# The second expert layer of a decoder: rows fetched by a table of places in place of rows scattered to slots

## The reference

```python
idx1 = jnp.argmax(gates, axis=-1)
mask1 = jax.nn.one_hot(idx1, nE)
idx2 = jnp.argmax(gates * (1.0 - mask1), axis=-1)
mask2 = jax.nn.one_hot(idx2, nE)
pos1 = jnp.cumsum(mask1, axis=0) - mask1
mask1 = mask1 * (pos1 < capacity)
pos2 = jnp.cumsum(mask2, axis=0) - mask2 + jnp.sum(mask1, axis=0, keepdims=True)
mask2 = mask2 * (pos2 < capacity)
...
expert_in = jnp.einsum('nec,nh->ech', dispatch, x)
hmid = jax.nn.silu(jnp.einsum('ech,ehf->ecf', expert_in, w1) + b1[:, None, :])
expert_out = jnp.einsum('ecf,efh->ech', hmid, w2) + b2[:, None, :]
y = jnp.einsum('nec,ech->nh', combine, expert_out)
shared = jax.nn.silu(x @ sw1 + sb1) @ sw2 + sb2
out = y + SHARED_SCALE * shared
```

## Time and profile before

| | |
|---|---|
| Time, median of 3 runs (lowest, highest) | 1610.15 us (1605.52, 1614.38) |
| The profiled execution: its time, its span | 1613.86 us, 1611.9 us |
| Busy share of the span: PE, PEld, DVE, ACT, POOL | 90%, 69%, 64%, 51%, 42% |
| Share of the chain that ended last, L2245 (the 28 scatters) | 8.8% of the chain's view by line |
| Span of the stage `experts1` | about 187 us, from 1425 us to the end |

### The profile page before, as it was taken

The page is one execution under the profiler, slowest core; times in us unless marked ns, Lnnn a source line. Parts: engine busy times, 40 slices in busy tenths (PEclk is TensorE's granted clock), DMA queues, the critical chain, the costliest instruction groups (busy, mean ns, idle before and its releaser), DMA issues. The chain is left out here.

```text
span 1611.9 us, 43113 instructions
## 1 busy us (share of the span) xinstructions
PE 1453.4 (90%) x16061; PEld 1116.6 (69%) x16061; DVE 1037.6 (64%) x1692; ACT 827.6 (51%) x1297; POOL 672.4 (42%) x732
## 2 busy tenths in 40 slices
PE   7988899989999987679999999999999999985684
PEld 4445676679999656357777777777777777764583
DVE  4334545668788559467777777777777777535362
ACT  5553333432222337436666666666666666654461
POOL 2300000477787546444433444334443344147263
PEclk9879999999999999789999999999999999987797
DMA  2064984131110320285556655666556655331402
GB/s 78 23 173 136 241 240 131 40 110 63 65 42 23 55 51 2 61 199 116 129 141 153 136 129 127 143 153 134 129 127 143 153 133 129 83 80 38 110 25 85
DMA packets 72884, 174.36 MB, mean 108 GB/s; under 512 B 14989, under 2 KB 44286, under 8 KB 72800
## 3 DMA queue, kind: packets, MB, share of 16 engines
q1 hardware_dynamic: 67936, 157.72, 40.1%
q10 hardware_dynamic: 2688, 11.78, 2.5%
q0 software_dynamic: 2176, 3.71, 0.7%
HBM read 87.58 MB, written 9.56 MB: 60 GB/s over the span
## 5 line engine op out<-in xcount | busy, mean ns | idle before, releaser
L2006 DVE TENSOR_REDUCE hat_tops<-banks 128x1 f32<-128x500 f32 x672 | 439.3, 676 | 153.1 <-PE banks L1751 153.0
L1879 ACT ACTIVATE hat_pb<-banks 125x896 f32<-125x896 f32 x384 | 340.3, 916 | 226.5 <-PE banks L1770 222.7
L1751 PE MATMUL banks<-hat_kh,hat_qm 128*128 128x500 f32 x672 | 298.1, 462 | 5.7 <-DVE hat_tops L2006 3.5
L1770 PEld LDWEIGHTS banks<-hat_q,hat_k 128*125 128x125 f32 x1536 | 219.8, 189 | 74.8 <-issue 32.4
L1770 PE MATMUL banks<-hat_q,hat_k 128*125 128x224 f32 x1536 | 250.8, 286 | 16.2 <-ACT hat_pb L1879 9.2
L1948 POOL CAST hat_kh<-hat_kf 128x500 fp32r<-128x500 f32 x96 | 58.5, 609 | 404.3 <-ACT hat_kf L1892 388.3
L1761 PE MATMUL banks<-hat_pb,hat_vs 125*27 125x168 f32 (+1 forms) x6144 | 166.9, 261 | 0.1
L1761 PEld LDWEIGHTS banks<-hat_pb,hat_vs 125*27 125x27 f32 (+1 forms) x6144 | 132.2, 98 | 43.9 <-issue 24.4
L1751 PEld LDWEIGHTS banks<-hat_kh,hat_qm 128*128 128x128 f32 x672 | 127.8, 192 | 47.4 <-DVE hat_tops L2006 32.8
L1315 ACT ACTIVATE ffn_rg<-banks 128x448 f32<-128x448 f32 x128 | 69.9, 546 | 166.2 <-PE banks L1248 166.0
L1954 POOL TENSOR_TENSOR hat_kl<-hat_kf,hat_kh 128x500 fp32r<-128x500 f32 x96 | 118.2, 1258 | 2.1 <-DMA hat_k<-hat_kh 2.1
(11 more groups left out here) (338 smaller groups left out, 2721.8 us busy)
## 6 DMA issues: line engine op xcount, KB each, us to landing
hat_k<-hat_kh SPq DMA_DIRECT2D x256, 187.5 KB, 4.8
hat_ct<-ctxT SPq DMA_DIRECT2D x32, 750.0 KB, 6.1
hat_k<-hat_kl SPq DMA_DIRECT2D x128, 187.5 KB, 4.5
ctx_cx<-ctx SPq DMA_DIRECT2D x32, 672.0 KB
ctx_cd<-ctxT ACTq DMA_DIRECT2D x15, 750.0 KB, 5.0
ffn_cb<-expert_weights SPq DMA_DIRECT2D x8, 896.0 KB, 4.4
moe_raw<-Mw SPq DMA_DIRECT2D x18, 256.0 KB, 4.0
ctx_cx<-ctx SPq DMA_DIRECT2D x32, 78.0 KB
```

Source lines behind the costliest of these rows:

```text
L1751: peak_out.inc(nc.tensor.matmul(g.bank(PK + m % 2)[:, 0:SB], qm[u][:].rearrange("p h i -> p (h i)")[:, r * 128:r * 128 + 128], kh[u][:, c ...
L1770: mm = nc.tensor.matmul(g.bank(2 * (t % 2) + j // 2)[0:SW, (j % 2) * QW:(j % 2 + 1) * QW], k3[u][:, j, t * SW:(t + 1) * SW], q3[u][:, j, : ...
L1879: exped.inc(nc.scalar.activation(pb[t % 6][:].rearrange("p (n i) -> p n i", n=2), g.ps[0:SW, 2 * (t % 2):2 * (t % 2) + 2, 0:2 * QW], ACT.E ...
L2006: peaked.inc(v.tensor_reduce(tops[:, r, n:n + 1], g.bank(PK + m % 2)[:, 0:SB], AX_X, ALU.max))
```

## The change

- The rows of tokens are stored once to memory (`rows`, 4 transfers of SyncE, in its queue behind the loads of the third set of weights), and GpSimd fetches an expert's rows straight from there by a list of token numbers, 128 rows an instruction: four instructions an expert and one more for each pair of experts, which holds the last 48 rows of both. That is 36 fetches in place of 28 scatters and 8 loads, and 36 sends in place of 40.
- The list is a table of places, made by matmuls. `on_pe_tally` sums each tile's choices, ScalarE copies the sums (`by_tile`), `on_pe_places` makes the places of both choices (six matmuls in place of VectorE's running sums), VectorE makes for each of the 28 tiles and choices a 128 by 128 matrix of zeros and ones (`lanes`, four instructions of 896 columns) and 36 columns of numbers (`tile_of`), and `on_pe_list` multiplies and adds up all 28. VectorE makes the numbers to fetch and to send from the sum (`name`).
- GpSimd's list: rows of experts 0 to 3, then in round e the results of e, then the rows of e+4. There are four buffers of rows (`ROWS`); the fetch of e+4 waits for `turn(e)`.
- TensorE's list: logits are made chunk by chunk inside the norm; six pieces up of the shared expert stand ahead of the list matmuls, and all 16 pieces down behind them, each with the piece up six further on.
- VectorE takes over from GpSimd the remainders of the first four pieces and of the stream (`low_x`), and gives to ScalarE the diagonals of shares (`lots`, 28 instructions of 128 columns, four in each round from 1 on, behind the round's other work). Copying an expert's rows out of PSUM takes one instruction on ScalarE and on VectorE instead of two, and `keep_out` two instead of one.
- Weights have four sets of buffers instead of six; two sets that were rounded during the shared expert are rounded in rounds 1 and 2. The rows loaded back at the end have four buffers, so no load waits for a matmul. Clearing `slot_rows` in an earlier stage goes away, and the constants are 292 columns wider.

```diff
+    def on_pe_tally(self, pe, bank):
         nc = self.g.nc
-        pe.wait_ge((self.one, self.two)[k], 1)
-        flat = self.hot[:, k].rearrange("p t e -> p (t e)")
-        nc.tensor.matmul(bank[:, 224 * k:224 * k + 112], self.g.c["before"], flat, start=True, stop=True)
-        nc.tensor.matmul(bank[:, 224 * k + 112:224 * k + 224], self.g.c["ones"], flat, start=True, stop=True).then_inc(self.tallied, 1)
+        pe.wait_ge(self.taken, 2)
+        for k in range(2):
+            flat = self.hot[:, k].rearrange("p t e -> p (t e)")
+            mm = nc.tensor.matmul(bank[0:TT * E, k * 128:k * 128 + 128], flat, self.g.c["ones"], start=True, stop=True)
+        mm.then_inc(self.summed, 1)
+
+    def on_act_tally(self, act, bank):
+        act.wait_ge(self.summed, 1)
+        self.g.nc.scalar.copy(self.by_tile[:], bank[0:TT * E, 0:256]).then_inc(self.summed_kept, 1)
...
+    def on_pe_places(self, pe, bank):
+        nc, c_ = self.g.nc, self.g.c
+        pe.wait_ge(self.summed_kept, 1)
+        for k in range(2):
+            at = k * (TT * E)
+            nc.tensor.matmul(bank[:, at:at + TT * E], c_["before"], self.hot[:, k].rearrange("p t e -> p (t e)"), start=True, stop=False)
+            nc.tensor.matmul(bank[:, at:at + TT * E], self.by_tile[:, k * 128:k * 128 + 128], c_["tiles_before"][0:TT * E, 0:TT * E], start=False, stop=True)
+        for k in range(2):
+            at = 2 * TT * E + k * E
+            mm = nc.tensor.matmul(bank[:, at:at + E], self.by_tile[:, k * 128:k * 128 + 128], c_["tiles_before"][0:TT * E, TT * E:], start=True, stop=True)
+        mm.then_inc(self.placed, 1)
+
+    def on_pe_list(self, pe, bank):
+        nc = self.g.nc
+        pe.wait_ge(self.tiled, 1)
+        for n in range(2 * TT):
+            if n % 7 == 0:
+                pe.wait_ge(self.laned, n // 7 + 1)
+            mm = nc.tensor.matmul(bank[:, 0:self.tiles], self.lanes[:, n, :], self.tile_of[:, n, :], start=(n == 0), stop=(n == 2 * TT - 1))
+        mm.then_inc(self.listed, 1)
...
+        bases(dve, places, bank[:, 2 * half:2 * half + E], bank[:, 2 * half + E:2 * half + 2 * E])
+        self.step(dve, v.tensor_tensor(self.counts[:], self.pos[:], self.hot[:], ALU.mult))
+        self.step(dve, v.tensor_reduce(self.row[:, 4:6, :], self.counts[:], AX_X, ALU.add))
+        flat = self.row[:, 4:6, :].rearrange("p k t -> p (k t)")
+        self.step(dve, v.tensor_scalar(self.start[:], flat, 128.0 * self.tiles - 63.5, GRAIN, ALU.add, ALU.add))
+        self.step(dve, v.tensor_scalar(self.start[:], self.start[:], GRAIN, None, ALU.subtract))
+        self.step(dve, v.scalar_tensor_tensor(out=self.lane[:], in0=flat, scalar=128.0 * self.tiles, in1=self.start[:], op0=ALU.add, op1=ALU.subtract))
+        self.step(dve, v.tensor_tensor(self.tile_of[:], spread(self.start[:], 2, self.tiles), spread(c_["tile_start"][:, 0:self.tiles], 1, 2 * TT), ALU.is_equal))
+        v.tensor_tensor(self.tile_of[:], self.tile_of[:], spread(c_["token_id"], 2, self.tiles), ALU.mult).then_inc(self.tiled, 1)
+        for n in range(4):
+            part = slice(7 * n, 7 * n + 7)
+            v.tensor_tensor(self.lanes[:, part, :], spread(self.lane[:, part], 2, 128), spread(c_["lane"], 1, 7), ALU.is_equal).then_inc(self.laned, 1)
...
+        self.step(dve, v.tensor_scalar(self.second[:], ids, float(NT - NOWHERE), float(NT), ALU.is_ge, ALU.mult))
+        v.scalar_tensor_tensor(out=self.fetch_id[:], in0=ids, scalar=float(NOWHERE), in1=self.second[:], op0=ALU.add, op1=ALU.subtract).then_inc(self.named, 1)
+        v.tensor_scalar(self.send_id[:], ids, float(NOWHERE), None, ALU.add).then_inc(self.named, 1)
...
-                    if s == SETS - 1:
-                        sp.wait_ge(sent_all, 16 * 2 * TT)
-                        for e in range(E):
-                            sp.dma_start(rows[e][:], g.slot_rows[e * CAPACITY:(e + 1) * CAPACITY].rearrange("(n p) c -> p n c", p=PART)).then_inc(rows_in[e], 16)
-                for e in range(E):
-                    sp.wait_ge(out_sent[e], 16 * 5)
...
+                    if s == RAWS - 1:
+                        for i, (a, b) in enumerate(GROUPS):
+                            sp.wait_ge(rows_kept, i + 1)
+                            sp.dma_start(g.rows[a * 128:b * 128].rearrange("(t p) d -> p t d", p=128), back[i][:, 0, 0:b - a, :]).then_inc(rows_stored, 16)
...
-                for i, (a, b) in enumerate(GROUPS):
-                    pool.wait_ge(rows_kept, i + 1)
-                    nc.gpsimd.tensor_copy(sent[:, 1, a:b, 0:D], sent[:, 0, a:b, 0:D]).then_inc(rows_doubled, 1)
-                for j in range(POOLED):
-                    pool.wait_ge(high0, j + 1)
-                    nc.gpsimd.tensor_tensor(ring0(hl, j), ring0(hf, j), ring0(hh, j).bitcast(F32), ALU.subtract).then_inc(low0_pool, 1)
...
-                    for t in range(TT):
-                        nc.gpsimd.indirect_dma_start(out=g.slot_rows, out_offset=bass.IndirectOffsetOnAxis(ap=pick.slot[:, k, t:t + 1], axis=0),
-                                                     in_=sent[:, k, t, :], in_offset=None, bounds_check=SLOTS - 1, oob_is_err=False).then_inc(sent_all, 16)
...
-                def send(e):
-                    pool.wait_ge(out_kept, e + 1)
-                    for n in range(5):
-                        nc.gpsimd.indirect_dma_start(out=g.token_rows, out_offset=bass.IndirectOffsetOnAxis(ap=rows[e][:, n, D:D + 1].bitcast(mybir.dt.int32), axis=0),
-                                                     in_=ow[e % 2][:, n, :], in_offset=None, bounds_check=2 * NT - 1, oob_is_err=False).then_inc(out_sent[e], 16)
...
+                def fetch(to, q, signal, n):
+                    nc.gpsimd.indirect_dma_start(out=to, out_offset=None, in_=g.rows, in_offset=bass.IndirectOffsetOnAxis(ap=pick.fetch_id[0:n, q:q + 1], axis=0),
+                                                 bounds_check=NT - 1, oob_is_err=False).then_inc(signal, 16)
...
+                def fetch_rows(e):
+                    if e >= ROWS:
+                        pool.wait_ge(turned, e - ROWS + 1)
+                    for n in range(4):
+                        fetch(rows[e % ROWS][:, n, :], tile_at(e, n), rows_in[e % ROWS], 128)
...
+                for e in range(4):
+                    fetch_rows(e)
+                    if e % 2 == 0:
+                        fetch_rest(e // 2)
                 for e in range(E):
-                    send(e)
+                    send_rows(e)
+                    if e % 2:
+                        m = e // 2
+                        send(rest_ow[m % 2][0:64 + REST, :], rest_at(m), rest_sent[m % 2], 64 + REST)
+                    if e + 4 < E:
+                        fetch_rows(e + 4)
+                        if e % 2 == 0:
+                            fetch_rest((e + 4) // 2)
...
-                norm.on_pe(pe)
-                pe.wait_ge(norm.normed, CH)
-                pe.wait_ge(norm.logged, CH)
-                pick.on_pe_logits(g.bank(3))
+                norm.on_pe(pe, lambda c: pick.on_pe_logits(g.bank(4), (0, 3, 7, 10)[c], (3, 7, 10, TT)[c]))
...
+                for j in range(4):
+                    up_shared(j)
+                pick.on_pe_tally(pe, g.bank(3))
+                up_shared(4)
+                pe.wait_ge(rows_kept, len(GROUPS))
+                pick.on_pe_places(pe, g.bank(2))
+                up_shared(5)
+                pick.on_pe_list(pe, g.bank(3))
+                for j in range(UN):
                     down_shared(j)
+                    if j + EARLY_UPS < UN:
+                        up_shared(j + EARLY_UPS)
...
                 def turn(e):
-                    pe.wait_ge(rows_in[e], 16)
+                    pe.wait_ge(rows_in[e % ROWS], 64 * (e // ROWS + 1))
+                    if e % 2 == 0:
+                        pe.wait_ge(rest_in[e // 2 % 2], 16 * (e // 4 + 1))
...
+                    for i in range(4 * (e - 1), 4 * e) if e >= 1 else ():
+                        k, t = divmod(i, TT)
+                        mul = nc.scalar.activation(lots[k][:, t, :], c_["ident"], ACT.Copy, scale=pick.share[:, k, t:t + 1])
...
-                    if e in (1, 2):
-                        dve.wait_ge(sent_all, 16 * 2 * TT)
-                        v.tensor_tensor(lots[:, e - 1], spread(c_["ident"], 1, TT), spread(pick.share[:, e - 1], 2, 128), ALU.mult).then_inc(lots_made, 1)
```

336 lines of the change are left out of this document (179 added, 157 removed).

## The result

The changed kernel takes 1621.5 us (median of 17 runs, 1614.99 to 1630.37) against 1606.9 of the kernel before (17 runs, 1601.29 to 1618.22) on the same chip: ratio 1.0085, 95% interval 1.0066 to 1.0103. It is slower by 0.85%, where 1604 us was predicted against 1610.15, which is 0.38% faster.

What follows compares the result with a forecast made beforehand. The scatters' end was taken to set the experts' start, then TensorE to pace. Loads back 5.3 us earlier and 1.3 in the joins make 6.6 less: 1610.15 to 1603.5, put at 1604, range 1594 to 1616.

Steps and rivals of the forecast that it cites:

- nine instructions of GpSimd: In each of four rounds, GpSimd's sends and fetches take 12.1 us, against 8.8 to 9.3 that TensorE needs.
- loads back: At the end, loading rows back starts at 1587.9, 5.3 us earlier than 1593.15, behind the sends of result 7.
- joins: At the end, four buffers let TensorE's 56 join passes run without the 1.34 us gap: 1.3 us won.
- rival A: The main forecast, with the list's 56 TensorE passes at half clock in 12.3 us: 1598 to 1611, chance 0.46.
- E: Early start not won: VectorE's table or handovers to the list take 4 to 8 us more; 1608 to 1615, chance 0.10.
- C: In the rounds, VectorE holds GpSimd up: at 1.90 us a step the 36 cost 20 us more; 1624, chance 0.14.
- D: In the rounds, GpSimd keeps pace: at 1.10 us or less a step, 8.6 us less; 1595, chance 0.10.
- From there GpSimd has 36 instructions before the rows of expert 7 are fetched: From result 0 on, GpSimd works 48.2 us at 1.34 each, without a pause, and rows come late.
- the last sum 1489.8: The shared expert's last sum ends at 1489.8, so turn 0 starts then, 11.4 us earlier than before.
- TensorE now arrives warm, which gives back 2.6: From turn 0 to result 0, TensorE starts at a higher clock, saving 2.6 of 22.1 us; result 0 out at 1509.3.
- Turn 7 starts at 1559.1: In the rounds, expert 7's turn starts at 1559.1, after result 0, GpSimd's 48.2 us and 1.6 us to land.
- I take the row of a send: A fetch's cost on GpSimd is taken from sends, as both move 128 rows through the same issuing engine: 1.34 us.

Runs made afterwards that it cites:

- no_round_fetch: The changed kernel without the 18 fetches of the rounds, experts 4 to 7 reusing rows of experts 0 to 3: ratio 0.9923 to the kernel before.
- plain_loads: The changed kernel with the rounds' 18 fetches replaced, in GpSimd's own list, by plain loads of 128 rows by position: ratio 0.9921 to the kernel before.
- before_fetch: The kernel before with 18 unused fetches of 112 rows added behind the sends of rounds 1 to 4: ratio 1.0211, silus 2.6 us late in sum.
- few_rows: The changed kernel with 16 rows instead of 128 in each of the rounds' 18 fetches: ratio 1.0145 to the kernel before.
- in_bounds: The changed kernel with empty places' fetch numbers lowered to 1791, so no row is skipped: ratio 1.0050 to the kernel before, silus 10.8 us late in sum.
- first_in_bounds: The changed kernel fetching e+4 ahead of sending e, empty places lowered to row 1791: ratio 1.0062 to the kernel before, silus 24.2 us late in sum.

## Why the prediction was wrong, step by step

Places of the changed kernel, moved by 4.3 us to the axis of the prediction:

| step | predicted | measured |
|---|---|---|
| logits done | 1437.6 | 1436.6 |
| places done | 1451.4 | 1447.8 |
| the list | 12.3 us | 12.13 us |
| list ended | 1470.7 | 1467.6 |
| first fetch | 1471.7 | 1469.1 |
| turn 0 | 1489.8 | 1491.8 |
| result 0 out | 1509.3 | 1514.5 |
| nine instructions of GpSimd | 12.1 us | 12.5 and 12.2 us |
| turn 7 | 1559.1 | 1579.2 |
| loads back | 1587.9 | 1609.2 |
| joins | 1.3 us won | gap gone |

**Right.** The list at half clock (rival A), the early start as far as the first fetch (E is refuted), GpSimd's price of a fetch, equal to a send's (1.00 and 0.30 where nothing disturbs it, 1.36 to 1.39 over a round), and with it that VectorE doesn't hold GpSimd up: C ended on the side that came true, by a mechanism that did not occur. D is refuted too: turns 4 and 6 wait 4.29 and 3.66 us, about the 3 that were forecast for turn 4; turns 5 and 7, which were to wait as well, don't wait for rows. The clock in the list depends on what TensorE did before it: idle for 6.98 us, then 12.13 us; busy for 9.18 us, then 6.38 us; busy for 6.18 and idle for 0.97, then 9.37 us. The Trainium skill says that sustained activity releases the throttle (TensorE: Matmul & The Clock Gate, Part 1, "What's actually happening"). The 9.18 us agree with that. The list itself doesn't: the granted clock stayed 0.50 through the 12.13 us and fell from 1.00 to 0.50 within the 9.37 us, though TensorE was busy throughout.

**Wrong: fetches cost GpSimd's time and nothing else.** The prediction doesn't say this, but its sum goes by it. The step that failed is that of the rounds, "From there GpSimd has 36 instructions before the rows of expert 7 are fetched", 48.2 us at a steady 1.34 each. The sum took fetches as instructions that cost GpSimd 1.34 us and hand over rows; nothing in it stood for what they do to TensorE's signals. That missing term hit three places. In the shared expert, "the last sum 1489.8": the last piece down is recorded to end at 1483.50 and its sum starts at 1486.74, behind 2.29 us in which VectorE idles for "remote"; turn 0 is 2.0 us late though the first fetch was 2.6 early and the list ended 3.1 early, so what lies between the list and turn 0 took 5.1 us more than in the sum; two late silus of 2.25 and 1.09 us stand in it as well. From turn 0 to result 0, "TensorE now arrives warm, which gives back 2.6": it idled 4.01 us for those sums and came cold (granted clock 0.50 from 1487.50 to 1496.00), 22.7 us instead of 19.5. In the rounds, "Turn 7 starts at 1559.1": it starts at 1579.2, behind two standstills in which TensorE idles for 7.08 and 7.20 us, and GpSimd, which should have paced the rounds without a pause, waits itself; from result 0 to the loads back are 94.7 us, not 78.6. The three (2.0, 3.2 and 16.1) make 21.3 us, the distance of the loads back from their predicted place. That all of it comes from the late signals is argued from the rows, not shown.

That it is the fetches is shown by taking them away (no_round_fetch, plain_loads). That fetches don't always do it is shown by before_fetch (2.6 us). That it is the signals that come late, in order, and not the matmuls is shown by the semaphore times of few_rows. What inside the chip holds them, and why the amount differs from run to run of like programs (in_bounds 10.8, first_in_bounds 24.2), stays open; fetches with another target than SBUF were not tried.

The rows that were shown held no warning of it: the trace before has no fetch by numbers into SBUF, only scatters out of it. The prediction says "I take the row of a send"; that bounded the price on the issuing engine, and I let it stand for all costs.

## What to carry to other kernels

An operation that the trace has never shown has a price on its own engine and a price on its neighbours; bound the second too, and where no row can, give it a chance with a time. When engines stand still together and the releaser is called "remote" or "issue", lay each waiting row beside the recorded end of what it waits for: a stretch of several microseconds between them is not a wait in the program. And replace the suspect by a plain transfer of the same bytes at the same place before turning orders around: one such run (plain_loads) told more than five rearrangements.
